# Windowed attention blocks on one core: attention output normalised by VectorE in 32 by 32 blocks, with three smaller moves in the order of work

## What is computed

```python
h = layernorm(x)
win = window_partition(h, 14)                    # padded to 28 x 28: 4 windows of 196 tokens per image
q, k, v = split(win @ qkv_w + qkv_b)             # 12 heads of 16 channels
attn = softmax(q @ k.T * 16**-0.5 + rel_h + rel_w)
out = (attn @ v) @ proj_w + proj_b
x = x + window_unpartition(out)
x = x + gelu(layernorm(x) @ w1 + b1) @ w2 + b2   # 192 -> 768 -> 192
```

## Time and profile before

| | |
|---|---|
| median of 3 runs | 676.68 us (676.61 to 677.33) |
| the profiled execution's own time | 682.86 us |
| its span in the profile | 681.1 us |
| busy TensorE matmul, weight load | 623.2 us (92%), 480.5 us (71%) |
| busy VectorE, ScalarE, GpSimd | 360.6, 334.0, 129.9 us |
| TensorE clock granted | 0.98 of full, mean over the span |

### The profile page before, as it was taken

One profiled execution on the slowest core, in us unless ns is written; L12 is line 12 of the kernel. 1 busy time (PEld: TensorE's weight loads), 2 busy tenths in 40 slices (PEclk: granted clock), 3 DMA queues, 4 the chain that ended last, 5 costly groups with the idle time before them and its releaser, 6 DMA issues.

```text
span 681.1 us, 14753 instructions
## 1 busy us (share of the span) xinstructions
PE 623.2 (92%) x5696; PEld 480.5 (71%) x5696; DVE 360.6 (53%) x989; ACT 334.0 (49%) x807; POOL 129.9 (19%) x172
## 2 busy tenths in 40 slices
PE   3799999999999999999999999999999999899996
PEld 2587776777677768775877587758775876477674
DVE  4447463746374637462655365546552764426665
ACT  3326743674367435744474447543744365315453
POOL 1800032003300330023002400140013000412220
PEclk9959999999999999999999999999999999799998
DMA  4774670067205720571047003700280000000000
GB/s 110 163 154 119 135 168 7 3 133 153 69 2 124 160 59 3 113 157 36 3 87 162 22 2 77 172 22 2 66 184 21 3 3 1 1 24 1 24 24 23
DMA packets 33175, 47.51 MB, mean 70 GB/s; under 512 B 5563, under 2 KB 14331, under 8 KB 33107
## 3 DMA queue, kind: packets, MB, share of 16 engines
q1 hardware_dynamic: 31874, 46.18, 29.5%
q10 hardware_dynamic: 1232, 0.40, 0.2%
HBM read 7.25 MB, written 1.57 MB: 13 GB/s over the span
## 4 chain that ended last, share of the span: by engine, by line
issue 55%; PE 25%; POOL 12%; DVE 4%; ACT 2%; DMA 1%; POOLq 0%; ACTq 0%; SPq 0%; DVEq 0%
POOL xn L821 4%; POOL q_nat L802 3%; PE bank L631 2%; PE bank L580 2%; PE bank L625 2%; PE bank L497 2%; PE bank L516 2%; PE bank L390 2%; PE bank L431 2%; POOL x_all L808 2%; POOL x_all L814 2%; POOL rstd L795 1%; PE bank L467 1%; PE bank L614 1%; PE bank L598 1%
## 5 line engine op out<-in xcount | busy, mean ns | idle before, releaser
L1268 ACT ACTIVATE PT<-bank 98x392 f32<-98x392 f32 (+1 forms) x288 | 136.8, 490 | 134.1 <-PE bank L497 130.0
L983 DVE TENSOR_REDUCE neg_max<-bank 98x2 f32<-98x392 f32 x192 | 106.4, 562 | 116.6 <-PE bank L467 116.1
L497 PE MATMUL bank<-q_aug,k_aug 127*98 127x196 f32 (+1 forms) x672 | 112.9, 264 | 0.9 <-ACT PT L1268 0.3
L467 PE MATMUL bank<-k_aug,q_aug 126*98 126x196 f32 x384 | 87.4, 314 | 11.2 <-DVE neg_max L983 9.6
L497 PEld LDWEIGHTS bank<-q_aug,k_aug 127*98 127x98 f32 (+1 forms) x672 | 88.0, 168 | 10.5 <-ACT PT L1268 5.8
L802 POOL TENSOR_TENSOR q_nat<-st_q 96x392 f32<-96x392 f32 (+2 forms) x48 | 24.9, 546 | 330.9 <-DVE st_q L951 330.9
L580 PE MATMUL bank<-w_down,PT 128*128 128x192 f32 x384 | 74.1, 330 | 7.0 <-ACT PT L1299 7.0
L467 PEld LDWEIGHTS bank<-k_aug,q_aug 126*98 126x98 f32 x384 | 56.1, 169 | 33.7 <-DVE neg_max L983 15.9
L390 PE MATMUL bank<-xT,w_qkv 97*96 97x256 f32 (+2 forms) x272 | 75.5, 393 | 1.8 <-ACT xT L1205 1.4
L580 PEld LDWEIGHTS bank<-w_down,PT 128*128 128x128 f32 x384 | 61.8, 190 | 8.7 <-ACT PT L1299 8.2
L981 DVE TENSOR_REDUCE neg_max<-bank 120x1 f32<-120x318 f32 x96 | 46.5, 485 | 33.5 <-PE bank L463 33.4
(11 more groups left out here) (97 smaller groups left out, 968.0 us busy)
## 6 DMA issues: line engine op xcount, KB each, us to landing
q_aug<-st_q SPq DMA_DIRECT2D x64, 192.0 KB
k_aug<-st_k SPq DMA_DIRECT2D x64, 192.0 KB, 5.0
q_aug<-st_r SPq DMA_DIRECT2D x64, 168.0 KB
x_all<-in_x SPq DMA_DIRECT2D x4, 384.0 KB, 5.9
q_aug<-negT ACTq DMA_DIRECT2D x96, 1.5 KB
k_aug<-st_p SPq DMA_DIRECT2D x16, 74.2 KB, 2.3
w_up<-in_w_up SPq DMA_DIRECT2D x2, 576.0 KB, 5.0
w_down<-in_down_w SPq DMA_DIRECT2D x4, 288.0 KB, 5.6
```

The source lines that it names most:

```text
L467: last = t_.matmul(b[0:HALF, WIN * r:WIN * r + WIN], q_aug[0:NEG, h, c + HALF * r:c + HALF * r + HALF], k_aug[0:NEG, h, c:c + WIN], start= ...
L497: last = t_.matmul(b[0:keys, m * k:m * k + m], k_aug[0:NEG + 1, h, c + keys * k:c + keys * k + keys], q_aug[0:NEG + 1, h, c:c + m], start= ...
L983: ins = v.tensor_reduce(neg_max[0:HALF, slot(n, u), e:e + 5:4], b[0:HALF, 0:2 * WIN] .rearrange("p (r m) -> p r m", r=2), AX.X, ALU.max, n ...
L1268: s.activation(PT[0:rows, i % 8, 0:m], bank[2 + i % 2][0:rows, 0:m], ACT.Exp).then_inc(S["exp"], 1)
```

## The change

The division is made without TensorE. `o_nat` keeps all three head groups. VectorE's `divide` turns each 32 by 32 block of a group's 128 x 512 tile (`o_turn`), takes 16 reciprocals per partition (`inv_sum`), multiplies in place (`o_div`), and turns the blocks back into `o_nat` (`oT`). It stands at steps (6, 2) and (7, 2) for groups 0 and 1, and after `k_low` for group 2. `transpose_o`, `transpose_out` and both `copy_oT` go. `project_out` takes `o_nat` directly: 4 token tiles by 3 groups of 128 rows, with `w_proj` padded with zero rows (128 x 3 x 192 in place of 96 x 2 x 192). Down product f of tile 0 waits for gelu tile f + 1 (at least 3), and the early scores move from behind products 1 and 4 to behind 3 and 5. `place_x` of VectorE issues its three instructions at steps (0, 1), (0, 2) and (0, 3). The four query pieces of half 1 stand at the four steps of unit 8.

```diff
@@ TensorE
-                    need(pe, ["xT_dve", "xT_act"][j], m, 1)
+                    need(pe, ["xT_dve", "xT_act"][j], m, [3, 1][j])
...
-                if u >= 7:
-                    need(pe, "o_tok", n, (u - 4) // 3)
-                else:
-                    need(pe, "o_tok", n - 1, 3)
                 t_.transpose(bank[5][0:66, 0:rows], neg_max[0:rows, slot(n, u), :], ident[0:rows, 0:rows])\
...
             def project_out(n, t):
                 l = layer(n)
                 if t == 0:
-                    need(pe, "oT_dve", n, 1)
-                    need(pe, "oT_act", n, 1)
+                    need(pe, "oT", n, 3)
+                    need(pe, "negT", n, UNITS)
+                    need(pe, "exp", n, HEADS)
                     pe.wait_ge(ld_back[l], LD_BACK)
-                for g in range(G):
-                    last = t_.matmul(bank[PROJ_BANK[t]][:, 0:C], yT[0:96, g, 128 * t:128 * t + 128],
-                                     w_proj[l][:, g, :], start=(g == 0), stop=(g == 1))
+                for hg in range(3):
+                    last = t_.matmul(bank[PROJ_BANK[t]][:, 0:C], o_nat[:, hg, 128 * t:128 * t + 128],
+                                     w_proj[l][:, hg, :], start=(hg == 0), stop=(hg == 2))
...
-                if t == 0 and f == 0:
-                    need(pe, "gelu", n, MC)
+                if t == 0 and f != 1 and f != 2:
+                    need(pe, "gelu", n, max(3, f + 1))
...
-                        if e == 2 and u >= 4 and u % 3 == 1:
-                            transpose_o(n, u // 3 - 1)
...
-                            if u == 8 and e in (0, 3):
-                                queries_in(n + 1, 1, e // 3, 1)
+                            if u == 8:
+                                queries_in(n + 1, 1, e, 1)
...
-                if more:
-                    queries_in(n + 1, 1, 2, 2)
                 for k in range(3):
                     values(n, LAST, k)
...
-                transpose_o(n, 2)
...
-                transpose_out(n)
...
-                        if more and f in (1, 4):
+                        if more and f in (3, 5):
                             early_scores(n + 1, 4 + 2 * t + f // 4)
@@ VectorE
-            def place_x(n):
+            def place_x(n, k):
...
-                for dst, src in pieces(xT[0:96, 0, 0:TOK], bank[front_bank(n, "x0")][0:96, :]):
-                    last = v.tensor_scalar(dst, src, affine[l][0:96, 0, 0:1], affine[l][0:96, 1, 0:1], ALU.mult, ALU.add)
-                last.then_inc(S["xT_dve"], 1)
+                dst, src = pieces(xT[0:96, 0, 0:TOK], bank[front_bank(n, "x0")][0:96, :])[k]
+                v.tensor_scalar(dst, src, affine[l][0:96, 0, 0:1], affine[l][0:96, 1, 0:1], ALU.mult, ALU.add)\
+                    .then_inc(S["xT_dve"], 1)
...
             def divide(n, hg):
-                need(dve, "ot_mm", n, hg + 1)
-                if hg == 0:
-                    need(dve, "oT_mm", n - 1, 2)
-                o = bank[5][:, :].rearrange("p (t e m) -> p t e m", t=TILES, e=4)
-                v.reciprocal(inv_sum[:, hg % 2, :, :], o[:, :, :, HD]).then_inc(S["inv_sum"], 1)
+
+                need(dve, "o_copy", n, 3 * hg + 3)
+                need(dve, "oT", n, hg)
+                v.transpose(o_tok[:, :, :].rearrange("p b e -> p (b e)"), o_nat[:, hg, :]).then_inc(S["o_turn"], 1)
+                need(dve, "o_turn", n, hg + 1)
+                v.reciprocal(inv_sum[:, :], o_tok[:, :, HD]).then_inc(S["inv_sum"], 1)
                 need(dve, "inv_sum", n, hg + 1)
-                v.tensor_tensor(o_tok[:, :, 64 * hg:64 * hg + 64].rearrange("p t (e c) -> p t e c", e=4), o[:, :, :, 0:HD],
-                                inv_sum[:, hg % 2, :, :].unsqueeze(3).to_broadcast([128, TILES, 4, HD]), ALU.mult)\
-                    .then_inc(S["o_tok"], 1)
-
-            def copy_oT(n):
-                need(dve, "oT_mm", n, 1)
-                v.tensor_copy(yT[0:96, 0, :], bank[2][0:96, :]).then_inc(S["oT_dve"], 1)
+                v.tensor_tensor(o_tok[:, :, 0:HD], o_tok[:, :, 0:HD], inv_sum[:, :].unsqueeze(2).to_broadcast([128, 16, HD]), ALU.mult)\
+                    .then_inc(S["o_div"], 1)
+                need(dve, "o_div", n, hg + 1)
+                v.transpose(o_nat[:, hg, :], o_tok[:, :, :].rearrange("p b e -> p (b e)")).then_inc(S["oT"], 1)
...
-                            if (u, e) == (0, 1):
-                                place_x(n + 1)
+                            if u == 0 and e:
+                                place_x(n + 1, e - 1)
...
+                        if (u, e) == (6, 2):
+                            divide(n, 0)
+                        if (u, e) == (7, 2):
+                            divide(n, 1)
-                    if u >= 4 and u % 3 == 1:
-                        divide(n, u // 3 - 1)
...
-                copy_oT(n)
@@ ScalarE
-                if u % 3 == 0:
-                    if hg >= 2:
-                        need(act, "ot_mm", n, hg - 1)
-                    else:
-                        need(act, "ot_mm", n - 1, 3 - hg)
+                if u == 0:
+                    need(act, "proj", n - 1, 4)
...
-                copy_oT(n)
@@ host
+    w_proj = np.zeros((2, 4, 32, 3, C), np.float32)
+    w_proj[:, :, 0:HD] = arrays["proj_w"].reshape(2, 3, 4, HD, C).transpose(0, 2, 3, 1, 4)
+    arrays["proj_w"] = w_proj.reshape(2, 128, 3, C)
```

More of the change, by code:

```diff
@@ L139, in program @@
         w_rel = [sb(f"w_rel{l}", [96, 2 * RT * HG]) for l in range(2)]
-        w_proj = [sb(f"w_proj{l}", [96, G, C]) for l in range(2)]
+        w_proj = [sb(f"w_proj{l}", [128, 3, C]) for l in range(2)]
         w_up = [sb(f"w_up{l}", [128, MC + MC // 2, 128]) for l in range(2)]
@@ L188, in program @@
                  "k_mm k_hi k_lo p_mm p_hi p_lo r_tok rt_copy r_mm r_hi r_lo v_mm v_copy s_mm max nt_mm negT st_mm exp pv "
-                 "o_copy ot_mm inv_sum o_tok oT_mm oT_dve oT_act proj x1 x1b x2_mm x2_dve x2_act up gelu down out "
+                 "o_copy o_turn inv_sum o_div oT proj x1 x1b x2_mm x2_dve x2_act up gelu down out "
                  "xb t_mm t_copy fwd xf_dve xf_act mix1 relu_act relu_dve mix2 over o2 inv fold unfolded").split()
@@ L269, in load_back @@
             def load_back(l):
-                load(w_proj[l][:, :, :], d["proj_w"][l].rearrange("(g p) n -> p g n", g=G), ld_back[l])
+                load(w_proj[l][:, :, :], d["proj_w"][l], ld_back[l])
                 load(b_down[l][:, :], d["down_b"][l].rearrange("(a n) -> a n", a=1).broadcast_to([128, C]), ld_back[l])
@@ L386, in project @@
                         front_free(n, use)
-                        need(pe, "xT_dve", n, 1)
+                        need(pe, "xT_dve", n, 3)
                         need(pe, "xT_act", n, 1)
@@ L519, in values @@
                     last.then_inc(S["pv"], 1)
[L521 to L524, removed]
-                else:
[L526 to L534, removed]
-                for g in range(G):
-                    for t in range(TILES):
-                        last = t_.transpose(bank[2 + g][0:96, 128 * t:128 * t + 128], o_tok[:, t, 96 * g:96 * g + 96], ident[:, :])
-                    last.then_inc(S["oT_mm"], 1)
             def project_out(n, t):
@@ L938, in normalise @@
                 last.then_inc(S["xn2"], 1)
-            def place_x(n):
+            def place_x(n, k):
                 l = layer(n)
-                need(dve, "xT_mm", n, 1)
-                need(dve, "v_mm", n - 1, 3)
-                dve.wait_ge(ld_front[l], LD_FRONT)
-                for dst, src in pieces(xT[0:96, 0, 0:TOK], bank[front_bank(n, "x0")][0:96, :]):
-                    last = v.tensor_scalar(dst, src, affine[l][0:96, 0, 0:1], affine[l][0:96, 1, 0:1], ALU.mult, ALU.add)
-                last.then_inc(S["xT_dve"], 1)
+                if k == 0:
+                    need(dve, "xT_mm", n, 1)
+                    need(dve, "v_mm", n - 1, 3)
+                    dve.wait_ge(ld_front[l], LD_FRONT)
+                dst, src = pieces(xT[0:96, 0, 0:TOK], bank[front_bank(n, "x0")][0:96, :])[k]
+                v.tensor_scalar(dst, src, affine[l][0:96, 0, 0:1], affine[l][0:96, 1, 0:1], ALU.mult, ALU.add)\
+                    .then_inc(S["xT_dve"], 1)
             def q_low(n, g):
@@ L1071, in _ @@
             normalise_first()
-            place_x(0)
+            for k in range(3):
+                place_x(0, k)
             norm_stats(1)
@@ L1272, in copy_o @@
                 need(act, "pv", n, u + 1)
-                if u % 3 == 0:
-                    if hg >= 2:
-                        need(act, "ot_mm", n, hg - 1)
-                    else:
-                        need(act, "ot_mm", n - 1, 3 - hg)
-                p = pieces(bank[4][:, :], o_nat[:, hg % 2, :])
+                if u == 0:
+                    need(act, "proj", n - 1, 4)
+                p = pieces(bank[4][:, :], o_nat[:, hg, :])
                 if window(u) == 2:
@@ L1285, in copy_o @@
                 last.then_inc(S["o_copy"], 1)
-            def copy_oT(n):
```

(2 more changed lines are left out.)

11 lines of the change are left out of this document (5 added, 6 removed).

## The result

The changed kernel took 684.28 us in the median of four runs (680.51 to 685.83) against 676.64 us: a ratio of 1.0088, 95% interval 1.0045 to 1.0131. Repeated (e1, twelve runs) it was 680.59 against 677.35 us, 1.0049 (1.0016 to 1.0082). It is slower, by 3 to 8 us; the forecast was 0.5 us faster.

The account below looks back on a forecast made before the run. TensorE's order, busy 92% of the span, was taken to set the time. Per job +0.85 - 1.1 = -0.25 us, seven jobs -1.75, last job +1.3: -0.45 in all, 676.2 us against 676.68; range 670 to 687.

Parts of the forecast that it names:

- Down: First down product of a job: its wait for gelu goes, 1.1 us less per job.
- Late queries: Two query pieces moved ahead of the last scores_T: TensorE then waits before the last value product, 0.45 us per job.
- Placing: Three placing steps in unit 0: the 1.13 us stall is cut in two, not shortened; gain 0.
- Division: Division on VectorE: 0.84 less in the loop, 0.4 back, 0.48 earlier at the projection, 1.33 for its third group.
- The wait at the query piece: Before unit 8's first query piece, TensorE waits 0.4 us for r_low, delayed on VectorE by divisions 0 and 1.
- projection +1.33: The projection has three head groups in place of two, 24 records for 16: 1.33 us longer.
- Rival (c): VectorE's block transpose costs more than an elementwise pass; each 0.1 us more costs 4.2 us in seven jobs; chance 0.27.
- Rival (b): TensorE's work decides: all savings come off, 2.3 us in each of seven jobs, 660 us; chance 0.08.
- -0.25 us; seven jobs -1.75: Sum per job, +0.85 at the projection and -1.1 at down, taken alike for seven jobs.
- No DMA is moved past another, the load is needed at the end of a job: Load of w_proj, twice as long, issued in the first job: put at nothing; if late, a cost once per layer.
- The last job: No query there and to_tokens covers the gelu wait, so no down gain; projection 1.33 us longer: +1.3 us.
- one of its signs of being wrong: A new wait in the last job, where VectorE has the shrinks beside division 0; no size given.

Follow-up runs that it names:

- e4: The kernel before with only the down products' waits per MLP tile and the early scores behind products 3 and 5; 667.79 us, ratio 0.9859.
- e3: The changed kernel with the two late query pieces back behind the last scores_T; 677.70 us, ratio 0.9994.
- e7: The changed kernel with the three placing instructions in one step again; 681.60 us, ratio 1.0016.
- e6: The kernel before with only the division on VectorE; placing, queries, down waits and early scores as before; 688.73 us, ratio 1.0121.
- e10: The changed kernel with the first block transpose of every division made twice; 737.54 us, ratio 1.0862.
- e2: The changed kernel with p_low ahead of the last division at the end of the fourth job; 680.59 us, ratio 1.0034.
- e5: The changed kernel with the last division of a job ahead of k_low on VectorE; 672.38 us, ratio 0.9890.
- e8: The changed kernel with the changes of e5 and e3 together, and the second division one step later, behind r_low; 667.24 us, ratio 0.9803.
- e11: e8 with the short placing instruction first and the first query piece one step later, at (1, 1); 665.33 us, ratio 0.9803.
- e12: The kernel before with one more load (128 KB, 32 KB for the second layer) ahead of the back weights; 679.18 us, ratio 1.0020.
- e9: The kernel before once more, unchanged; 677.03 us, profiled span 675.2 us.

## Why the prediction was wrong

**The ordinary job was right in every step.** Down: 1.1 predicted, 1.2 measured (e4). Late queries: +0.45, 0.45 (e3). Placing: 0, 0.1 at most (e7). Division: +0.4 by the terms, 0.5 (e6). The wait at the query piece was 0.4, and is 0.34; projection +1.33: it takes 4.0 us (228.26 - 224.26) for 2.67. The block transpose was put at 0.68, and takes 0.70 and 0.71; six of them in the chain would make the 0.15 us between the period predicted (68.75) and found (68.9), though smaller misses in the other terms are as large. Rival (c)'s mechanism is real (e10 shows its slope), but its price did not come: 0.70 to 0.71 us makes about 1 us in seven jobs by that slope. (One slip in its use: a transpose of 0.59 us would by it lower the sum by 3.8 us, not some 3.) Rival (b), that TensorE's work decides, fell with e6.

**The sum failed at "seven jobs" (the step "-0.25 us; seven jobs -1.75").** The fourth job is not like the others. It has `p_low` behind the division on VectorE, and I counted what waits behind the division only for the ordinary job, where `r_low` and `add_projection` have time. There the prediction said "they come no later than the longer projection"; for `p_low` it is false: TensorE waited 1.57 us for it. With it went the second thing that the prediction did not have at all, the clock. It fell in four of the five profiled executions that have the 1.57 us wait (after, e1, e6, e7; not e3; e10 is left out, its clock falls in every period from the second on), and in the fourth job of none of the four that lack it (e2, e5, e8, e11). I had priced such stalls as plain idle time. Queue and clock together are +2.9 and +4.1 us in the two executions (73.7 and 74.9 against 70.8); e2 takes both away, e3 shows the queue without the clock.

**"No DMA is moved past another, the load is needed at the end of a job"** was the wrong question. TensorE never waits for the load itself, but for another transfer. First job: +0.4 to +0.8 us (69.6, 70.0 against 69.2), and e12 shows the same, 1.1 us, from a load alone.

**The last job was put too dear.** +1.3 us predicted. The rest of the span is 209.0 us in e4 and 210.6 in e1, neither with a fallen clock before its last 4 us: 1.6 more. But the rest holds the seventh period too, an ordinary one, 67.8 in e4 and 68.9 in e1. That is 1.1 of the 1.6, so the last job itself lost 0.5. From the start of the projection to the end of the span it is 1.3 us longer (100.3 for 99.0), as predicted. Ahead of the projection it is 0.8 shorter, which the prediction had at nothing, although one of its signs of being wrong came true: TensorE waits 1.43 us for a spectral instruction of VectorE, queued behind the last division. The rows are of TensorE and VectorE in the last job of the changed kernel:

```profile
577.17 1.38 PE L603 MATMUL bank<-w,o 128*72 128x96 f32 x14 [1.43 <-DVE o L1011]
578.38 4.09 PE L525 MATMUL bank<-w_proj,o_nat 128*128 128x192 f32 x24
```

```profile
576.00 0.71 DVE L980 STREAM_TRANSPOSE o_nat<-yT 128x512 f32<-128x512 f32 x1
576.64 0.48 DVE L1011 TENSOR_SCALAR o<-bank,b 128x288 f32<-128x288 f32 x1
```

Together, e1 against e9: fourth +4.1, first +0.4, the four ordinary periods -0.3, the seventh -0.1, last +0.5. The last job's part does not show in these two spans, because e9 has a fallen clock there (rest 211.6). The medians say +3.2 and +7.6. What stays open is how much of the latter is a matter of which launches had the clock fall at the start or the end: each kernel has such launches, and that the change makes them more frequent is not shown by these samples.

## What to carry to other kernels

A sum per period times the number of periods needs a look at the odd period: list what else stands on the queue there, behind each instruction that grew. Where an engine idles ahead of an instruction that waits for another engine, put the long independent chain into that gap, not behind it; here two exchanged lines were worth 1.0 us of 68.9. And a bundle is to be taken apart: one part of this one gave 1.2 us a job, one took 0.5, one 0.45, and the whole looked like nothing.

## What the runs showed of the hardware

- A VectorE block transpose of 128 x 512 fp32 takes 0.70 to 0.71 us, 0.02 to 0.03 more than an elementwise pass of as many elements (0.68). In the Trainium skill (Vector Engine (DVE) Microarchitecture Reference, section on the reshape front-end) it sustains one element per cycle per lane. The traces fit that, in that the transpose costs what one elementwise pass costs; no run varies its length.
- The price of a stall of TensorE can have a step. Waits of 0.34 to 0.73 us, four of them between 213.9 and 224.3 us, left the clock alone in every ordinary job of the profiled executions. With one of 1.57 us behind ones of 1.17 and 0.73 the grant fell to 0.50 in four executions (after, e1, e6, e7) and not in a fifth (e3). With one of 1.83 us in e10 it was at half for some 20 us, though TensorE was busy for 8.79 of the 10 us before; in the first job of the same execution waits of 1.85 and 1.47 us left it at full. There 1.5 us of VectorE work before each query piece, and 0.7 before the projection, cost 57 us against e1, where the waits alone would be 15 to 20. What decides between the two outcomes stays open.
- Stalls of 1.13 and 1.00 us in every ordinary job of the kernel before, at places where TensorE is otherwise full, cost no clock in its two profiled executions.
- A transfer of 1.5 KB made TensorE wait 1.1 us with 128 KB more of weights under way (e12), and not at all in two executions without them (before, e9).
